# Splitting W1 into high and low parts: one expert in each of eight batches, or four experts in each of two

## The reference

```python
h = _layernorm(x) * (1 + ca) + sa
Q = h @ Wq + bq                       # K = V = Q
x = x + ga * (softmax(Q @ Q.T / sqrt(128)) @ Q)
h = _layernorm(x) * (1 + cb) + sb
route = sigmoid(h @ Wr + br)          # 8 experts; the largest one takes the token
for e in range(8):
    mask = (argmax(route) == e)
    y = gelu(h @ W1[e]) @ W2[e]       # W1: 8 x 128 x 512, W2: 8 x 512 x 128
    out = out + mask * y
x = x + gb * out * max(route)
```

## Time and profile before

| | us |
|---|---|
| median of 3 runs (351.85 to 352.88) | 352.49 |
| the profiled execution: its own time | 352.24 |
| the profiled execution: span from first to last instruction | 350.5 |
| PE busy | 325.7 (93% of the span) |
| DVE busy | 277.5 (79%) |
| ACT busy | 222.6 (63%) |
| POOL busy | 191.5 (55%) |

### The profile page before, as it was taken

How to read it: one execution, slowest core, us unless ns; L and a number is a source line. 1 busy time by engine, 2 the same in 40 slices (tenths; PEclk the granted TensorE clock), 3 DMA queues, 4 the chain that set the end, 5 groups by cost and what they waited for, 6 DMA issues and landing times.

```text
span 350.5 us, 8421 instructions
## 1 busy us (share of the span) xinstructions
PE 325.7 (93%) x2580; PEld 300.1 (86%) x2580; DVE 277.5 (79%) x1115; ACT 222.6 (63%) x476; POOL 191.5 (55%) x224
## 2 busy tenths in 40 slices
PE   3899999999999999999989898899999999999960
PEld 3587888889888988898878798899999999999960
DVE  4479898898889888988997886899887677778730
ACT  2588987798779877987775586654445444334310
POOL 4018456645664566446624546777666556565661
PEclk9999999999999999999999999999999999999995
DMA  3294135528763858753636613564999554354300
GB/s 114 81 291 112 34 65 119 145 104 101 150 125 102 111 131 210 212 147 118 110 80 238 233 47 79 188 209 135 298 278 283 164 176 126 113 145 121 93 21 4
DMA packets 34349, 49.21 MB, mean 140 GB/s; under 512 B 4304, under 2 KB 25971, under 8 KB 34304
## 3 DMA queue, kind: packets, MB, share of 16 engines
q1 hardware_dynamic: 27328, 31.66, 38.9%
q0 software_dynamic: 6368, 16.92, 13.0%
q10 hardware_dynamic: 608, 0.08, 0.1%
HBM read 28.15 MB, written 20.96 MB: 140 GB/s over the span
## 4 chain that ended last, share of the span: by engine, by line
PE 69%; DVE 13%; ACT 6%; issue 5%; DMA 2%; DVEq 1%; SPq 1%; POOL 1%; POOLq 0%; ACTq 0%
PE mixed L633 14%; PE mixed L533 12%; PE flipped L520 6%; PE side L483 4%; PE scores L510 3%; PE scores L508 3%; PE scores L509 3%; PE side L553 3%; PE scores L617 2%; PE scores L618 2%; PE side L465 2%; PE scores L616 2%; PE side L545 2%; PE flipped L616 2%; PE flipped L618 2%
## 5 line engine op out<-in xcount | busy, mean ns | idle before, releaser
L1426 POOL DMA_INDIRECT sorted_rows<-payload,slots x64 | 63.8, 996 | 79.5 <-DVE slots L1064 64.5
L1453 POOL DMA_INDIRECT out_dram<-y_out,tokens x71 | 73.8, 1039 | 43.5 <-DVE y_out L1125 27.9
L633 PE MATMUL mixed<-down_slot,hidden 128*128 128x128 f32 x568 | 70.2, 276 | 2.5 <-ACT hidden L819 2.5
L633 PEld LDWEIGHTS mixed<-down_slot,hidden 128*128 128x128 f32 x568 | 66.5, 192 | 3.0 <-ACT hidden L819 3.0
L533 PE MATMUL mixed<-v_sb,probs_t 128*128 128x128 f32 x512 | 69.0, 278 | 0.0
L762 ACT ACTIVATE probs<-scores,row_max 128x512 f32<-128x512 f32 x64 | 43.9, 687 | 34.7 <-DVE row_max L957 33.2
L533 PEld LDWEIGHTS mixed<-v_sb,probs_t 128*128 128x128 f32 x512 | 62.2, 192 | 0.2
L957 DVE TENSOR_REDUCE row_max<-scores 128x1 f32<-128x512 f32 x64 | 44.0, 688 | 19.0 <-PE scores L510 18.9
L804 ACT ACTIVATE f_hi<-side 128x256 fp32r<-128x256 f32 (+1 forms) x39 | 14.2, 365 | 42.7 <-PE side L595 38.5
L520 PE MATMUL flipped<-ident,probs 128*128 128x128 f32 x256 | 39.1, 275 | 0.6 <-ACT probs L762 0.5
L770 ACT ACTIVATE probs_t<-flipped 128x512 f32<-128x512 f32 x64 | 37.8, 593 | 0.0
(11 more groups left out here) (190 smaller groups left out, 769.0 us busy)
## 6 DMA issues: line engine op xcount, KB each, us to landing
rows<-sorted_rows SPq DMA_DIRECT2D x32, 388.0 KB, 3.8
x_tile<-in_L_attn_inputs_dram SPq DMA_DIRECT2D x16, 256.0 KB, 3.2
payload<-stored_gates SPq DMA_DIRECT2D x16, 256.0 KB, 9.6
sorted_rows<-pad_rows SPq DMA_DIRECT2D x9, 388.0 KB, 4.6
w_parts<-in_L_ffn_W_dram SPq DMA_DIRECT2D x1, 2048.0 KB, 10.2
rows<-sorted_rows SPq DMA_DIRECT2D x7, 194.0 KB, 2.8
out_dram<-y_out,tokens POOLq DMA_INDIRECT x71
sorted_rows<-payload,slots POOLq DMA_INDIRECT x64, 5.0
```

Of the source, the lines that this page charges most:

```text
L633: last = nc.tensor.matmul(mixed[t % 2][:, u * H:(u + 1) * H], hidden[:, t % 2, f, u * P:(u + 1) * P], down_slot[:, t % 3, f, :], start=(f ...
L1426: nc.gpsimd.indirect_dma_start(rows_dram, bass.IndirectOffsetOnAxis(ap=slots[:, c:c + 1], axis=0), payload[:, b.q, j, :], None).then_inc(s ...
L1453: nc.gpsimd.indirect_dma_start(out_rows, bass.IndirectOffsetOnAxis(ap=tokens[:, t % RING, u:u + 1], axis=0), y_out[:, t % RING, u, :], Non ...
```

## The change

The table that tells in which slots which experts of W1 are split. Before, slot 0 splits experts 0 to 3 and slot 1 experts 4 to 7. Now slot k splits expert k, for k = 0 to 7. Number, shape and place within a slot of the instructions stay as they are.

```diff
-        W1_SPLITS = {k: range(k * E // 2, (k + 1) * E // 2) for k in range(2)}
+        W1_SPLITS = {k: (k,) for k in range(E)}
```

## The result

The changed kernel takes 358.56 us (median of 6 runs, 357.12 to 358.92), the kernel before 352.46 (6 runs, 351.66 to 352.94): ratio 1.0164, 95% interval 1.0145 to 1.0183. It is 6.1 us slower. The profiled execution took 358.62 with a span of 356.9; TensorE's granted clock was 0.987. In one later series of runs the kernel before itself took 368 us in place of 352, at a granted clock of 0.967 to 0.982, so the three experiments of that series were run a second time and only those second runs are compared with others.

The account below looks back on a forecast made before the run. PE was taken to bound the kernel (69% of what ended last). The terms -2.3 + 1.3 + 5 x 1.41 = +6.0 us led from a profiled 352.24 to 358.5 us by median (chance 0.73), range 355.8 to 361.2.

Parts of the forecast that it names:

- The mechanism: Slots 2 to 8: POOL's subtraction waits for ACT's copy ahead of the scatter; the lateness goes round, PE waits; +6.0 us overall.
- What goes: Slots 1 and 2: one copy in place of four gives back nearly all their excess, 2.3 us.
- ACT's copies: Slots 2 to 7: one added copy each, 0.55 us, costs nothing by itself because PE's own work covers it.
- The entry: End of slot 3: the first late scatter makes PE stand still for 1.3 us.
- The turn: From one POOL subtraction to the next: 13.16 us against PE's 11.75, so PE waits 1.41 in each.
- the upper bound: Turning slots: L1396 takes 1.33 us instead of 1.01 if it meets something else, 6 x 0.32 = 1.9 us more.
- Five turns and an end behind slot 8: From slot 2's split to slot 7's: five turns at 1.41 us each, the last showing at slot 8's end.
- The rule on the port: DVE and POOL lock a shared port pair, the second blocks; spread subtractions just miss L889, sum stays +6.0 us.
- The rival in which the delay is absorbed: POOL's delay in the slots costs nothing, the burst was the whole cost: 350.2 us, chance 0.05.
- the one in which it is paid once: A turn shorter than PE's 11.75 us, so only the entry counts: 351.5 us, chance 0.05.
- The longer turn of 13.5: L1396 at 1.33, a subtraction meeting DVE's port, or PE slow to restart: 360.4 us, chance 0.17.
- the ring: Chain POOL, DVE, ACT and back to POOL's next subtraction, put at 13.16 us against PE's 11.75.

Follow-up runs that it names:

- the second subtraction: The changed kernel with a second subtraction of the same shape, into a scratch tensor, behind each of the eight on POOL: 365.23 us, ratio 1.0376.

## Why the prediction was right

The forecast was 358.5 us, measured were 358.56; the sum was +6.0, the trace's account is +5.97. The mechanism is the forecast one; that the two numbers agree to a tenth is luck, since the terms are off by 0.1 to 0.3 each with both signs, and 0.4 of the spans' difference has no name. By its steps:

- *What goes* was put at 2.3 and is 2.20. That it would be nearly all of the excess was right. The prediction left open which burst makes it; the runs without subtraction say 0.5 by ACT and 1.7 by POOL.
- *ACT's copies* at nothing: right, by the run without subtraction.
- *The entry* was put at 1.3 and is 1.44. The first DMA started 51.77, 4.32 after `flip_xn`, as worked out (4.39). It lasted 1.20 instead of 1.06. I had counted only on L545's wait; L717 let PE wait too, in this slot and in each turn, for `offset1` was late. Behind these waits the transposes at L465 take 0.66 and those at L545 0.63, instead of 0.60.
- *The turn* was put at 13.16, measured 13.10 (52.39 us from 63.57 to 115.96, four turns). Its terms were off in ways that nearly cancel: the gap in front of the DMAs 0.17 for 0.30, against the subtraction 1.28 for 1.25 and L1396 1.05 for 1.01. The first turn, 50.30 to 63.57, took 13.27.
- *L1396* took 1.05 in the turning slots, near the 1.01 that I took and far from the 1.33 of the upper bound.
- *Five turns and an end behind slot 8*: right, slot 9 takes 11.79 between its `flip_xn2`s and slot 10 is 11.75. The turns were put at 5 x 1.41 = 7.05 and are 6.73.
- *The rule on the port*, weighed and found without effect on the sum: right for this kernel, where L889 starts at 77.92 as the subtraction ends at 77.95, and takes 0.17. It is a close miss, and the run with the scatter first shows what a meeting costs there: 0.85 in each slot.

The rival in which the delay is absorbed falls with the trace of the changed kernel; the one in which it is paid once falls with its five equal turns and with the second subtraction. The longer turn of 13.5 didn't come either. What is shown: the ring needs both the wait for ACT and the scatter behind it, since taking away either opened it (352.75 and 355.13), and wait and order keep it going with almost no work in the subtraction (357.19 with 8 columns). What isn't shown alone is the length of each link.

## What to carry to other kernels

An instruction given to an idle engine isn't free if it waits there: ask what stands behind it in that engine's order, who waits for that, and whether the chain comes back to what it waits for within one round of the loop. Such a ring costs its excess over the bound in each round, here 1.44 us once and 1.35 five times, though no engine is clearly fuller than before (POOL is busy for 53% of the span, before 55%). In this kernel spreading the burst was worth its gain only where each piece found its input ready and held up nothing on DVE's way to PE; a lag of one slot and a wait that sets the place did that.

## What the runs showed of the hardware

A DVE instruction on four numbers per partition can be stopped while POOL subtracts. With the scatter first, L992 (128x4) took 1.78 to 1.81 us instead of 0.17 in slots 3 to 8 and ended with the subtraction beside it, though it started 0.45 to 0.48 us before the subtraction, while POOL issued a DMA. In the kernel before, L889 (128x4) took 1.14 us beside the four subtractions.

An indirect DMA's issue on POOL took 1.42 to 1.45 us instead of 0.96 in five slots of the run with 8 columns, where DVE's L936, with two inputs in SBUF, had started 0.07 to 0.10 us before it. In the run with two subtractions it took 1.43 us where the same instruction started 0.08 us ahead of it, and 0.96 us where that instruction started 0.12 us after it (68.61 and 68.49).

In the turns the gap between a subtraction and the first indirect DMA behind it was 0.17 us after one of 1.28 us, and 0.63 after one of 0.20.
